# The second norm's transposes move into the queries' bank, and their copies move behind the queries' copy

## What is computed

```
x = x + xattn0(ctx, layernorm(x))      # 16 heads of 16; queries from x, keys and values from ctx
x = x + ffn0(layernorm(x))             # 8 experts; gate, top 2 counted, all experts weighted by the counts
x = x + xattn1(layernorm(x), ctx, mask)
x = x + ffn1(layernorm(x))             # 8 experts, top 2 of each token
```

## Time and profile before

| | |
|---|---|
| runs | 985.58, 985.85, 989.25 us; median 985.85 us |
| profiled execution | 987.03 us, its span 984.9 us |
| granted TensorE clock, mean | 0.958 of 2.4 GHz |
| busy over the span | TensorE 91%, VectorE 74%, GpSimd 56%, ScalarE 55% |

### The profile page before, as it was taken

The page is one execution under the profiler, slowest core; times in us unless marked ns, Lnnn a source line. Parts: engine busy times, 40 slices in busy tenths (PEclk is TensorE's granted clock), DMA queues, the critical chain, the costliest instruction groups (busy, mean ns, idle before and its releaser), DMA issues. The chain is left out here.

```text
span 984.9 us, 31478 instructions
## 1 busy us (share of the span) xinstructions
PE 900.4 (91%) x10664; PEld 668.7 (68%) x10664; DVE 730.3 (74%) x2071; ACT 543.4 (55%) x1068; POOL 551.4 (56%) x897
## 2 busy tenths in 40 slices
PE   4799999999999999986999999999976399999993
PEld 2477777777777777754466666666644289889892
DVE  6688888888888888866778888888865356666773
ACT  3377777777777777654044444444443065555551
POOL 6655555565555555401037777777776535556536
PEclk9899999999999999987999999999996599999997
DMA  5644554445444454331565555665552348786535
GB/s 157 178 128 142 144 147 134 135 144 147 125 139 141 142 142 144 94 105 47 141 179 174 183 186 186 189 191 184 175 190 90 120 100 197 176 187 105 96 64 59
DMA packets 107278, 140.56 MB, mean 143 GB/s; under 512 B 23929, under 2 KB 92592, under 8 KB 106928
## 3 DMA queue, kind: packets, MB, share of 16 engines
q1 hardware_dynamic: 94594, 121.38, 41.3%
q0 software_dynamic: 12528, 17.18, 9.7%
HBM read 93.38 MB, written 38.35 MB: 134 GB/s over the span
## 5 line engine op out<-in xcount | busy, mean ns | idle before, releaser
L999 DVE TENSOR_REDUCE smax<-psum 112x2 f32<-112x750 f32 x240 | 216.3, 933 | 24.5 <-PE psum L439 24.4
L840 ACT ACTIVATE probsT<-psum 125x896 f32<-125x896 f32 x173 | 158.7, 917 | 22.0 <-PE psum L454 20.6
L2035 POOL DMA_INDIRECT out_dram<-y,token_at x63 | 101.6, 1612 | 93.9 <-DMA out_dram<-y,token_at 42.2
L1733 DVE SCALAR_TENSOR_TENSOR acc<-psum,neg_bias,acc 128x448 f32<-128x448 f32 x112 | 75.9, 680 | 10.9 <-PE psum L1556 9.3
L1475 POOL DMA_INDIRECT dispatch_dram<-rows,slots_at x64 | 64.0, 1000 | 28.4 <-issue 28.4
L439 PE MATMUL psum<-k_stack,q_stack 63*128 63x375 f16 x480 | 69.3, 326 | 3.9 <-DVE smax L999 2.8
L1556 PE MATMUL psum<-xT_hi,we_hi 128*128 128x448 f16 x256 | 70.2, 356 | 1.1 <-ACT we_hi L1655 1.1
L476 PE MATMUL psum<-probsT,v_aug 125*32 125x112 f32 x2688 | 70.2, 260 | 0.1
L1556 PE MATMUL psum<-xT_lo,we_hi 128*128 128x448 f16 x256 | 69.8, 355 | 0.0
L1556 PE MATMUL psum<-xT_hi,we_lo 128*128 128x448 f16 x256 | 69.7, 354 | 0.0
L476 PEld LDWEIGHTS psum<-probsT,v_aug 125*32 125x32 f32 x2688 | 63.5, 110 | 8.9 <-ACT v_aug L866 8.5
(11 more groups left out here) (298 smaller groups left out, 2448.3 us busy)
## 6 DMA issues: line engine op xcount, KB each, us to landing
k_stack<-k_hi_dram SPq DMA_DIRECT2D x64, 188.0 KB, 2.8
we<-in_ctxT_dram SPq DMA_DIRECT2D x32, 375.0 KB, 3.5
ctxT<-in_ctxT_dram SPq DMA_DIRECT2D x32, 375.0 KB
ctx_rows<-in_ctx_dram SPq DMA_DIRECT2D x32, 375.0 KB
w_raw<-in_w_dram SPq DMA_DIRECT2D x32, 256.0 KB, 3.9
rows_e<-dispatch_dram SPq DMA_DIRECT2D x24, 272.0 KB
k_hi_dram<-k_hi SPq DMA_DIRECT2D x32, 188.0 KB, 2.8
k_lo_dram<-k_lo SPq DMA_DIRECT2D x32, 188.0 KB, 2.7
```

The costliest lines, as they stand in the source:

```text
L840: nc.scalar.activation(probsT[:, p, c, hg, :, :, :].rearrange("p k h q -> p k (h q)"), psum[0:KC, 0:2, 0:4 * S], ACT.Exp, scale=float(HD) ...
L999: nc.vector.reduce_max(smax[:, (u - LAG_B) % 2, 2 * (s % 4) + s // 4::PAIRS], psum[0:S, pair_bank(s):pair_bank(s) + 2, 0:KV], AX.X).then_i ...
L1733: nc.vector.scalar_tensor_tensor(out, psum[:, mix_bank(t, u, k), 0:GT], neg_bias[:, hc, e:e + 1], out, ALU.max, ALU.add).then_inc(m["acc_r ...
L2035: nc.gpsimd.indirect_dma_start(dram["out"], bass.IndirectOffsetOnAxis(token_at[:, unit // PAIR % TOKEN_TURNS, unit % PAIR:unit % PAIR + 1] ...
```

## The change

TensorE's two transposes of the second norm no longer stand ahead of pair scores 2 with bank 4 as their place, but behind transposed scores 0 with columns 256 to 479 of bank 6 (`NORM2_AT = D`), directly ahead of the query matmuls, which use columns 0 to 223 of that bank. The heads' four transposes move behind the query matmuls. ScalarE's copy of the high half moves behind the copy of the queries, with a further wait for the queries (`q_done`). VectorE's subtraction keeps its place in its stream and reads bank 6. Pair scores 3 no longer wait for the low half; the first key matmuls do, since they write columns 0 to 374 of bank 6. The transposes wait for the values of the step before to be copied out of bank 6 (`v_ready`) instead of for a maximum.

```diff
+    NORM2_AT = D
@@ scores
-                elif s == 3 and on[4]:
-                    wait(pe, m["x1lo_ready"], count(t, u - LAG_E, 1, 1))
@@ norm_turned_back
                     wait(pe, m["x1n_ready"], count(t, u - LAG_E, 1, 1))
-                    wait(pe, m["max_done"], count(t, u - LAG_B, PAIRS, 2))
+                    wait(pe, m["v_ready"], count(t, u - 1, 2, 1))
                     for kc in range(DC):
-                        last = nc.tensor.transpose(psum[:, 4, kc * S:(kc + 1) * S], x1n[:, kc * 128:(kc + 1) * 128], ident[0:S, 0:S])
+                        last = nc.tensor.transpose(bank_a[:, NORM2_AT + kc * S:NORM2_AT + (kc + 1) * S], x1n[:, kc * 128:(kc + 1) * 128], ident[0:S, 0:S])
@@ keys, mc == 0
                         wait(pe, m["qfull_ready"], count(t, u, 1, 1))
+                        if e:
+                            wait(pe, m["x1lo_ready"], count(t, u - LAG_E, 1, 1))
@@ TensorE's step
+                pair_scores(2)
+                unit_scoresT(0)
                 if e:
                     norm_turned_back()
-                pair_scores(2)
-                unit_scoresT(0)
+                new_queries()
                 if d:
                     heads_back()
-                new_queries()
                 unit_scoresT(1)
@@ ScalarE's step
-                if e:
-                    wait(act, m["x1nT_done"], count(t, u - LAG_E, 1, 1))
-                    nc.scalar.activation(xT_hi[:, :, bass.ds(be * S, S)], psum[:, 4, 0:DC * S].rearrange("p (c s) -> p c s", c=DC),
-                                         ACT.Copy).then_inc(m["x1hi_ready"], 1)
                 unit_exp(0)
...
                 nc.scalar.activation(q_full[:].rearrange("p c s -> p (c s)"), bank_a[:, 0:DC * S], ACT.Copy).then_inc(m["qfull_ready"], 1)
+                if e:
+                    wait(act, m["x1nT_done"], count(t, u - LAG_E, 1, 1))
+                    wait(act, m["q_done"], count(t, u, 1, 1))
+                    nc.scalar.activation(xT_hi[:, :, bass.ds(be * S, S)], bank_a[:, NORM2_AT:NORM2_AT + DC * S].rearrange("p (c s) -> p c s", c=DC),
+                                         ACT.Copy).then_inc(m["x1hi_ready"], 1)
                 unit_exp(1)
@@ VectorE's step
-                    nc.vector.tensor_tensor(xT_lo[:, :, bass.ds(be * S, S)], psum[:, 4, 0:DC * S].rearrange("p (c s) -> p c s", c=DC),
+                    nc.vector.tensor_tensor(xT_lo[:, :, bass.ds(be * S, S)], bank_a[:, NORM2_AT:NORM2_AT + DC * S].rearrange("p (c s) -> p c s", c=DC),
```

## The result

| | before | after |
|---|---|---|
| runs | 11, median 987.92 us | 11, median 995.1 us (990.57 to 1000.56) |
| ratio after to before | | 1.0082, 95% interval 1.0061 to 1.0102 |
| profiled execution | 987.03 us, span 984.9 | 994.24 us, span 992.0 |
| TensorE busy, 60 to 400 us | 339.74 us | 333.53 us |
| ordinary step of the loop | 12.97 us | 13.185 us |

The change makes the kernel slower by 0.8%, 7.2 us between the medians; the forecast was 13.5. The direction and the place were right, the size forecast was nearly double the measured one.

The account below looks back on a forecast made before the run. TensorE was taken to bound the first stage, with no slack for VectorE at the sixth maximum. Lateness 0.70 less 0.20 swallowed gives 0.50 us, times 27 steps 13.5 us; 985.85 + 13.5 = 999.4 us, range 989 to 1006.5.

Parts of the forecast that it names:

- The bound: First stage: TensorE, busy 339.74 of 340.00 us, bounds the loop; the sixth maximum's edge to the eighth pair has no slack.
- The clock: TensorE's clock was to stay 1.00, busy near 327 us; a rival had it fall, 1022 us, chance 0.04.
- The chain to the subtraction: Scores, norm's transposes, queries, ScalarE's two copies, VectorE's subtraction: at V+4.71 instead of V+4.01 (V: weighted values' start), 0.70 us later.
- The slack: VectorE's 0.20 us wait for the heads' high half swallows that much lateness, leaving 0.50 us at the sixth maximum.
- Where it bites: TensorE's pair scores: sixth pair 0.37 us late, part of the 0.50 us at the eighth, which waits for the sixth maximum.
- The keys' wait: First key matmuls wait for the subtraction until V+5.15, standing 0.08 to 0.13 us (bounds 0 and 0.2).
- "Inside" the other: The first key matmuls' wait lies within the 0.50 us, since VectorE's lateness overtakes it at the sixth pair.
- The switch saved: TensorE's new order has one switch of shape between matmuls fewer, worth some 0.05 to 0.12 us a step.
- The third rival: Not slower: the saved switch decides, steps 0.06 to 0.16 us shorter, 981.5 to 984.2 us, say 983; chance 0.08.
- its main term: The loop is longer by 0.50 us in each of 27 steps through VectorE's lateness, 13.5 us in all.

Follow-up runs that it names:

- the later subtraction: The changed kernel, but VectorE makes the heads' reciprocal and product first and the norm's subtraction behind them, ahead of the fourth maximum: 13.46 us a step, 997.77 us.

## Why the prediction was right, and what in it was too large

**The bound.** Right: in this stage TensorE has next to no idle time before, and the fourth and sixth maximum are what a late VectorE meets first. The clock stayed at 1.00, with TensorE busy 333.53 of 340 us (327 had been said).

**The chain to the subtraction, 0.70 us.** It came out at 0.57: V+4.58. The terms: scores to the norm's transposes 0.46 for 0.50, transposes 0.25 for 0.29 (the low end, half of the four, was the nearer), queries to their copy 0.79 as taken, copy to copy 0.26 for 0.31, copy to subtraction 0.38 as taken. Three of the five were a little large, all in one direction. The first was the distance to the heads' transposes in the longer step. The copy to copy was the distance to an exponential that had to wait (exponential 1 starts 0.31 behind the queries' copy, but its own scores, started at 264.25 and 0.37 long, end only 0.04 ahead of it).

**The slack, 0.20 us.** This is the term that was mis-sized most: it measures 0.36. The forecast counted only the idle time that a row prints. Two things were missing. The fourth maximum did not start straight behind the product: in an ordinary step of before 0.40 us lie between the two starts (277.40 to 277.80; 0.43 in the step of the earlier trace rows) and 0.34 in the changed kernel (267.90 to 268.24), so 0.06 of it was a wait, for the fourth pair's scores by the order of the step, that no row names. The rows on VectorE, before (V = 272.81) and changed:

```profile
277.40 0.42 DVE L1080 TENSOR_TENSOR o_nat<-psum,inv_sum 112x256 f32<-112x256 f32 x1
277.80 1.79 DVE L999 TENSOR_REDUCE smax<-psum 112x2 f32<-112x750 f32 x2
279.78 0.39 DVE L1097 TENSOR_TENSOR onT_lo<-psum,onT_hi 128x224 f16<-128x224 f32 x1 [0.20 <-ACT onT_hi L897]
280.09 0.93 DVE L999 TENSOR_REDUCE smax<-psum 112x2 f32<-112x750 f32 x1
```
```profile
267.90 0.42 DVE L1082 TENSOR_TENSOR o_nat<-psum,inv_sum 112x256 f32<-112x256 f32 x1
```

And an instruction of VectorE that waits for nothing, and does not read what the one before it wrote, mostly starts 0.07 to 0.09 us ahead of the printed end of that one (268.24 + 1.77 = 270.01, next start 269.94). So the heads' low half had been held back by 1.98 − 1.70 = 0.28 us between starts, not by the printed 0.20. With 0.02 more behind it the lateness at the sixth maximum is 0.57 − 0.06 − 0.28 − 0.02 = 0.21 us, against 0.50 forecast; with the forecast's 27 steps that is 5.8 us instead of 13.5. Of the 0.29 too much, 0.13 came from the chain and 0.16 from the slack.

**Where it bites.** Said: 0.37 at the sixth pair and 0.50 at the eighth. Measured: the sixth pair's scores at V+6.50 instead of V+6.30, 0.20, the eighth at V+8.49 instead of V+8.27, 0.22. So nearly all comes in at the sixth pair, and the eighth is nearly in time by itself.

**The keys' wait.** It was put at 0.08 to 0.13 us, at most 0.2, and measured at 0.21. When the keys are released was forecast well (V+5.12 for V+5.15); what was off is when TensorE comes to them: by itself it would at V+4.91, not at V+5.02 to V+5.07, since the order saves time ahead of them. "Inside" the other was right: without it the sixth pair's scores would still stand until V+6.50. What was missed is that it is the next bound: keys at V+5.12 would let the sixth pair start at V+6.37 (1.25 later), so 0.13 us more of it and it leads, as the later subtraction showed.

**The switch saved.** The order of the change saves 0.13 us a step. The place of the norm's transposes alone is worth 0.07 of it, inside the 0.05 to 0.12 said, and the rest comes with the heads' transposes behind the queries, which the forecast gave nothing. The 0.33 from which the upper end was taken stood in the longer step; it is 0.29 in ordinary ones. The Trainium skill's rule ("TensorEngine Tiling (Array Packing)", "Tiling Modes") agrees with the two kernels in which nothing else stands in the way: with one switch fewer their steps are 0.075 and 0.135 us shorter. That it is the switch, and not the order of the matmuls in some other way, no run separates. The third rival had the right mechanism, and the change loses it to the waits.

**Missed altogether.** The late transfer of the negated maxima, about 1.1 us. The prediction moved the first transposed scores forward by 0.34 us and asked only what follows them, not for what they wait.

**The sum after.** Ordinary steps 26 × 0.215 = 5.6, the two late steps 1.1, other uneven steps 0.1, together 6.8 in the loop; the two profiled spans differ by 7.1 and the medians by 7.2. That the measured time is no farther from the forecast is in part luck: the transfer, which the forecast did not have, fills up some of what its main term had too much.

## What to carry to other kernels

Where an engine is full and a neighbour is late, count the slack between starts, not by the printed idle time: compare each distance with the shortest distance of the same pair of shapes anywhere in the trace. Before a step is taken as the pattern, check that it is an ordinary one: here it was 0.04 us longer than most, which is a fifth of the effect. An instruction that is moved forward needs its own inputs checked, transfers above all, and not only its followers. When a move on the full engine saves time and its copies are put off to fit, look for an order that has the first without the second: here keeping the norm in its own bank, copied first, and moving the next transposed scores behind two pairs turned +0.8% into −0.35%.

## What the runs showed of the hardware

- Two transposes between the weighted values and the pair scores took 0.34 us; put directly ahead of the heads' transposes 0.27, directly ahead of the queries 0.25. With the first place the step was 0.075 us shorter, with the second, and the heads' transposes behind the queries, 0.135.
- Eight transposed scores take 0.21 us up to the next pair scores and 0.29 up to transposes or key matmuls.
- With waits of 0.34 us in each step of 13.2 the granted clock of TensorE stayed at its upper level of 2.4 GHz from 60 to 400 us of the changed kernel (1.00).
- A VectorE instruction not held by a wait mostly starts 0.07 to 0.09 us ahead of the printed end of the one before. Where it reads what that one wrote it starts later: the product 0.03 us behind the end of its reciprocal, a norm's aggregation 0.14 behind the end of its statistics.
- A small transfer issued at the same place of every step, V−0.83, let its reader start at V+2.61 in most steps of the changed kernel and only at V+3.53 in one.
